# A mixture-of-experts kernel: routing sums and tables in another order, the scatters in another order, fewer table steps, longer warm-up

## What is computed

```python
x = x + xattn(_layernorm(x), ctx, ctx, lens, ...)
xf = _layernorm(x)                                   # 2048 tokens, 256 wide
probs = softmax(einsum('td,ed->te', xf, gate_w))     # 8 experts
weights, idx = top_k(probs, 2)
weights = weights / sum(weights)
x1 = silu(einsum('td,efd->tef', xf, w1))             # 512 wide
x3 = einsum('td,efd->tef', xf, w3)
out_all = einsum('tef,edf->ted', x1 * x3, w2)
x = x + einsum('tkd,tk->td', take(out_all, idx), weights)
```

## Time and profile before

| | us |
|---|---|
| median of 3 runs | 1250.87 (1248.97 to 1251.0) |
| profiled execution | 1252.28 |
| its span in the profile | 1250.5 |
| TensorE busy | 1092.7 (87%) |
| VectorE busy | 978.4 (78%) |
| ScalarE busy | 729.5 (58%) |
| GpSimd busy | 654.2 (52%) |

### The profile page before, as it was taken

One profiled execution on the slowest core, in us unless ns is written; L12 is line 12 of the kernel. 1 busy time (PEld: TensorE's weight loads), 2 busy tenths in 40 slices (PEclk: granted clock), 3 DMA queues, 4 the chain that ended last, 5 costly groups with the idle time before them and its releaser, 6 DMA issues. The chain is left out here.

```text
span 1250.5 us, 33103 instructions
## 1 busy us (share of the span) xinstructions
PE 1092.7 (87%) x13015; PEld 711.6 (57%) x13015; DVE 978.4 (78%) x1781; ACT 729.5 (58%) x1297; POOL 654.2 (52%) x466
## 2 busy tenths in 40 slices
PE   1455999999999999999999999999978945999996
PEld 0322556656656656655665665666647942666663
DVE  5835899899999989989999999989944763555553
ACT  2522666666666666666666666666644642555553
POOL 1043684486477367448647746844349544333332
PEclk9656999999999999999999999999998976999999
DMA  8024232423333253242333324316636522333330
GB/s 271 1 54 104 77 85 57 123 71 96 87 89 82 62 130 84 62 109 75 91 94 89 86 70 114 86 41 182 206 113 236 169 86 76 56 50 55 52 59 11
DMA packets 103968, 117.03 MB, mean 94 GB/s; under 512 B 47293, under 2 KB 86014, under 8 KB 102526
## 3 DMA queue, kind: packets, MB, share of 16 engines
q1 hardware_dynamic: 91406, 100.46, 28.9%
q0 software_dynamic: 7152, 8.43, 4.0%
q10 hardware_dynamic: 5248, 5.92, 1.6%
HBM read 39.46 MB, written 36.87 MB: 61 GB/s over the span
## 5 line engine op out<-in xcount | busy, mean ns | idle before, releaser
L771 ACT ACTIVATE prob<-sc,key_bias 128x512 f32<-128x512 f32 x640 | 404.8, 684 | 149.4 <-PE sc L634 145.6
L852 DVE TENSOR_REDUCE part_max<-mx 128x1 f32<-128x427 f32 x768 | 418.4, 592 | 49.8 <-PE mx L646 49.8
L949 POOL TENSOR_TENSOR prob_lo<-prob 128x1024 bf16<-128x1024 f32 x128 | 242.2, 1893 | 240.3 <-ACT prob L771 240.3
L864 DVE TENSOR_TENSOR prob_lo<-prob 128x1024 bf16<-128x1024 f32 x192 | 274.7, 1431 | 10.8 <-ACT prob L771 7.2
L673 PE MATMUL pv<-VV,prob 128*128 128x65 bf16 x2560 | 268.0, 193 | 3.7 <-POOL prob_lo L949 3.5
L675 PE MATMUL pv<-VV,prob_lo 128*128 128x65 bf16 x2560 | 269.3, 195 | 0.0
L674 PE MATMUL pv<-VV,prob 128*128 128x64 bf16 x2560 | 268.0, 193 | 0.0
L673 PEld LDWEIGHTS pv<-VV,prob 128*128 128x128 bf16 x2560 | 239.8, 99 | 38.8 <-POOL prob_lo L949 7.3
L674 PEld LDWEIGHTS pv<-VV,prob 128*128 128x128 bf16 x2560 | 237.2, 97 | 26.5
L646 PE MATMUL mx<-K,Q 128*128 128x427 bf16 x768 | 237.2, 350 | 11.4 <-DMA K<-we 6.1
L633 PE MATMUL sc<-Q,K 128*128 128x512 bf16 x640 | 243.6, 381 | 1.3 <-ACT prob L771 1.3
(11 more groups left out here) (182 smaller groups left out, 1453.8 us busy)
## 6 DMA issues: line engine op xcount, KB each, us to landing
expert_inputs<-zeros SPq DMA_DIRECT2D x129, 129.0 KB, 2.8
Q<-we SPq DMA_DIRECT2D x48, 256.0 KB, 4.0
we<-in_w_exp SPq DMA_DIRECT2D x8, 1536.0 KB, 8.3
q32s<-q SPq DMA_DIRECT2D x128, 64.0 KB, 2.0
attention_out<-o_out SPq DMA_DIRECT2D x64, 128.0 KB, 1.9
o_in<-attention_out SPq DMA_DIRECT2D x16, 512.0 KB, 3.8
K<-we SPq DMA_DIRECT2D x48, 160.0 KB, 3.8
VV<-next_v SPq DMA_DIRECT2D x16, 322.5 KB, 4.1
```

Source lines behind the costliest of these rows:

```text
L771: act.activation(prob[:, s % PRING, j, :], sc[n % 2][:], ACT.Exp, bias=key_bias[:, t:t + 1], scale=HD ** -0.5).then_inc(exp_done, 1)
L852: dve.tensor_reduce(part_max[:, b_ % 2, qt, h:h + 1], mx[:, pl.part_banks(qt, h)[0]:pl.part_banks(qt, h)[-1] + 1, 0:pl.width], mybir.AxisL ...
L864: dve.tensor_tensor(prob_lo[:, s % PRING, 0:g, :], prob[:, s % PRING, 0:g, :], hi_half(prob[:, s % PRING, 0:g, :])[:, :, 1::2], ALU.subtra ...
L949: pool.tensor_tensor(prob_lo[:, s % PRING, 0:g, :], prob[:, s % PRING, 0:g, :], hi_half(prob[:, s % PRING, 0:g, :])[:, :, 1::2], ALU.subtr ...
```

## The change

The change touches four engines.

- *TensorE.* `places` is split into `places_from` (earlier tiles) and `places_within` (the batch's own), `counts` into tiles 0 to 11 and 12 to 15. Of batch 3 only the own part and the last four counts wait for its choice. `warm_up` has 17 products instead of 9 and doesn't wait for the low scatters.
- *VectorE.* Both choices lie in one tile `picks`, so that `place` has one product and one reduce for both; the minimum and maximum are written as whole numbers at once. `weights` is split into `shares`, `weigh_low` and `weigh_high`. `shares(3)` and `weigh_high(2)` move between `choose(3)` and `place(3)`, `weigh_high(3)` behind the tables. The tables (`tables`, before `owners`) have 14 steps instead of 19, and where two steps don't depend on each other the first is not waited for (`note`).
- *GpSimd.* Batch 1's high scatters move behind batch 3's low ones. The last twelve high scatters go in bursts of four, each waiting for the ones before.
- *SyncE* waits for `tables_made`, reads the entries of two tiles, loads these, and then reads and loads tile by tile.

```diff
@@ SyncE
-                sp.wait_ge(owner_made, 1)
+                sp.wait_ge(tables_made, 2)
                 sp.sem_inc(load_turn, 1)
-                first = [place_of(i) for i in range(TURN)]
+                first = [place_of(i) for i in range(2)]
                 for c in range(CH):
                     sp.wait_ge(scattered_low[c], 16 * QT)
-                for i in range(TURN):
+                for i in range(2):
                     fetch(i, *first[i])
+                for i in range(2, TURN):
+                    fetch(i, *place_of(i))
...
@@ GpSimd
-                def scatter_high(c, paced=False):
+                def set_high(c):
                     pool.wait_ge(scattered_low[c], 16 * QT)
                     pool.wait_ge(high_weighted, c + 1)
                     pool.tensor_copy(row_weights[:, batch(c)], high_weight[:, batch(c)]).then_inc(high_weights_set, 1)
                     pool.wait_ge(high_weights_set, c + 1)
-                    for t in range(c * QT, (c + 1) * QT):
-                        if paced and t % 2 == 0:
+
+                def scatter_high(tiles_, paced=False):
+                    for t in tiles_:
+                        if paced and t % QT == 0:
                             pool.wait_ge(scattered_high, 16 * t)
...
+                EARLY = QT
                 for c in range(CH - 2):
                     scatter_low(c)
-                    scatter_high(c)
+                    set_high(c)
+                    scatter_high(range(c * QT, min((c + 1) * QT, EARLY)))
                 for c in range(CH - 2, CH):
                     scatter_low(c)
...
+                scatter_high(range(EARLY, 2 * QT), True)
                 for c in range(CH - 2, CH):
-                    scatter_high(c, True)
+                    set_high(c)
+                    scatter_high(range(c * QT, (c + 1) * QT), True)
...
@@ VectorE
-                    for k in range(2):
-                        then(dve.tensor_tensor(g8[k][:], slot_of[:], pick[k][:], ALU.mult))
-                        then(dve.tensor_reduce(slot_f[:, k, :], g8[k][:], AX_X, ALU.add))
-
-                    then(dve.tensor_tensor(slot_f[:, 2, :], slot_f[:, 0, :], slot_f[:, 1, :], ALU.min))
-                    then(dve.tensor_tensor(slot_f[:, 3, :], slot_f[:, 0, :], slot_f[:, 1, :], ALU.max))
-                    dve.tensor_copy(slot[:, :, batch(c)], slot_f[:, 2:4, :]).then_inc(slots_made, 1)
...
+                    then(dve.tensor_reduce(slot_f[:].rearrange("p k t -> p (k t)"),
+                                           picked_slots[:].rearrange("p k t e -> p (k t) e"), AX_X, ALU.add))
+
+                    dve.tensor_tensor(slot[:, 0, batch(c)], slot_f[:, 0, :], slot_f[:, 1, :], ALU.min).then_inc(slots_made, 1)
+                    dve.tensor_tensor(slot[:, 1, batch(c)], slot_f[:, 0, :], slot_f[:, 1, :], ALU.max).then_inc(slots_made, 1)
+                    note(dve.tensor_tensor(first_low[:, c % 2, 0, :], slot_f[:, 0, :], slot_f[:, 1, :], ALU.is_lt))
+                    then(dve.tensor_tensor(first_low[:, c % 2, 1, :], slot_f[:, 0, :], slot_f[:, 1, :], ALU.is_gt))
...
                 place(2)
-                weights(2)
+                shares(2)
+                weigh_low(2)
                 keep_logits(3)
                 choose(3)
+                shares(3)
+                weigh_high(2)
                 place(3)
-                weights(3)
-                owners()
+                weigh_low(3)
+                tables()
+                weigh_high(3)
...
@@ TensorE
-                places(3)
                 pe.wait_ge(x1_made, ST)
-                for t in range(ST):
-                    ins = pe.matmul(counts, ones_b[:], chosen[:, t, :], start=t == 0, stop=t == ST - 1)
-                ins.then_inc(counted, 1)
+                count_tiles(range(0, 3 * QT))
+                pe.wait_ge(pc_read, 3)
+                places_from(3, range(3 * QT), True)
+                pe.wait_ge(chosen_made, 4)
+                places_within(3, False)
+                count_tiles(range(3 * QT, ST)).then_inc(counted, 1)
...
                 pe.wait_ge(owner_made, 1)
-                pe.wait_ge(scattered_low[CH - 1], 16 * QT)
-                warm_up(9)
+                warm_up(17)
```

More of the change, by code:

```diff
@@ L1498, in owners, with weigh_high, tables @@
+                def weigh_high(c):
+                    note(dve.tensor_tensor(ew_part[:, 2, :], ew[:, c % 2, 2, :], first_low[:, c % 2, 1, :], ALU.mult))
+                    then(dve.tensor_tensor(ew_part[:, 3, :], ew[:, c % 2, 3, :], first_low[:, c % 2, 0, :], ALU.mult))
+                    dve.tensor_tensor(high_weight[:, batch(c)], ew_part[:, 2, :], ew_part[:, 3, :], ALU.add).then_inc(high_weighted, 1)
+                def tables():
                     dve.wait_ge(counted, 1)
-                    then(dve.tensor_copy(count[:], counts))
@@ L1512, in owners @@
-                    then(dve.tensor_copy(owner[:], owner_f[:, 1, :]))
+                    dve.tensor_scalar(scatters[:], tile_numbers[0:1, :], tiles[0:1, 2, 0:1], 1.0, ALU.is_ge, ALU.add).then_inc(tables_made, 1)
+                    dve.wait_ge(picked, chain[0])
                     then(dve.tensor_tensor(skipped[:], ended[:, :, 0:E - 1],
                                            tiles[0:1, 3, 0:E - 1].unsqueeze(1).to_broadcast([1, MT, E - 1]), ALU.mult))
-                    then(dve.tensor_reduce(row_f[:, 0, :], skipped[:], AX_X, ALU.add))
@@ L1517, in owners @@
-                    then(dve.scalar_tensor_tensor(out=row_f[:, 1, :], in0=tile_numbers[0:1, :], scalar=float(P), in1=row_f[:, 0, :],
+                    note(dve.tensor_reduce(row_f[:, 0, :], skipped[:], AX_X, ALU.add))
+                    then(dve.tensor_reduce(owner_f[:], ended[:], AX_X, ALU.add))
+                    note(dve.scalar_tensor_tensor(out=row_f[:, 1, :], in0=tile_numbers[0:1, :], scalar=float(P), in1=row_f[:, 0, :],
                                                   op0=ALU.mult, op1=ALU.add))
-                    then(dve.tensor_scalar(row_f[:, 2, :], row_f[:, 1, :], float(E * S), None, ALU.min))
@@ L1520, in owners @@
-                    then(dve.tensor_copy(tile_row[:], row_f[:, 2, :]))
-                    then(dve.tensor_scalar(scatter_f[:, 0, :], tile_numbers[0:1, :], tiles[0:1, 2, 0:1], None, ALU.is_ge))
-                    then(dve.tensor_scalar(scatter_f[:, 1, :], scatter_f[:, 0, :], 1.0, None, ALU.add))
-                    dve.tensor_copy(scatters[:], scatter_f[:, 1, :]).then_inc(owner_made, 1)
+                    dve.tensor_scalar(owner[:], owner_f[:], float(E - 1), None, ALU.min).then_inc(owner_made, 1)
@@ L1526, in _ @@
+                    dve.wait_ge(picked, chain[0])
+                    dve.tensor_scalar(tile_row[:], row_f[:, 1, :], float(E * S), None, ALU.min).then_inc(tables_made, 1)
                 for step in range(STEPS):
@@ L1552, in _ @@
                     if step in (2 * QT + 3, 3 * QT + 3):
-                        weights((step - 3) // QT - 2)
+                        shares((step - 3) // QT - 2)
+                        weigh_low((step - 3) // QT - 2)
+                        weigh_high((step - 3) // QT - 2)
                     if step == ST + 1:
@@ L1611, in _, with mine, places_from, places_within @@
             def _(pe):
+                def mine(c):
+                    return pc[:, c * QT * E:(c + 1) * QT * E]
+                def places_from(c, tiles_, start):
+                    for t in tiles_:
+                        pe.matmul(mine(c), ones_b[:], chosen[:, t:t + 1, :].to_broadcast([P, QT, E]),
+                                  start=start and t == tiles_.start, stop=False)
+                def places_within(c, start):
+                    pe.matmul(mine(c), before_b[:], chosen[:, batch(c), :].rearrange("p t e -> p (t e)"), start=start, stop=False)
+                    for t in range(c * QT, (c + 1) * QT - 1):
+                        ins = pe.matmul(mine(c)[:, (t + 1 - c * QT) * E:QT * E], ones_b[:],
+                                        chosen[:, t:t + 1, :].to_broadcast([P, (c + 1) * QT - 1 - t, E]),
+                                        start=False, stop=t == (c + 1) * QT - 2)
+                    ins.then_inc(pc_ready, 1)
                 def places(c):
```

88 lines of the change are left out of this document (42 added, 46 removed).

## The result

| | before | changed |
|---|---|---|
| median (us) | 1250.76 (1248.97 to 1251.0) | 1242.18 (1241.82 to 1243.91, 4 runs) |
| ratio | 1 | 0.9944 [0.9929, 0.9960] |
| span of the profiled execution | 1250.5 | 1242.1 |

Faster by 8.6 us by the medians and by 7.0 by the ratio. The prediction was 1239.4 with a range of 1235.5 to 1243: right in direction and in what sets the end, 2.8 us too fast by the median and 4.5 by the ratio (0.9944 x 1250.87 = 1243.9, just outside the range). One term of its sum was too small, the waits between bursts of scatters.

The account below looks back on a forecast made before the run. Everything between the last routing batch and TensorE's first real tile was taken as exposed. Afterwards the stores set the end: first store -9.8, chain -1.7, so 1250.87 - 11.5 = 1239.4 us, range 1235.5 to 1243.

Parts of the forecast that it names:

- Earlier batches, -0.5: VectorE's batch 1 weights ahead of the residual add lose three chained steps: 0.5 us saved, ends 0 and -0.7.
- VectorE's steps (-1.5, -2.6, -1.5): Savings in us: batch 2 from place to next logits; batch 3's wait between choice and place; batch 3 from place to low weights.
- tables (6.0 to 4.0): VectorE's stretch from batch 3's low weights to finished tables shrinks from 6.0 to 4.0 us.
- The stall, taken as 0: Part of VectorE's 3.83 us wait for batch 3's sums might travel to the remaining matmuls: bounds 0 and +2.4 us.
- First load -12.9: SyncE's first tile load, released by batch 3's low scatters, comes at 1032.4 instead of 1045.35 us.
- Warm-up -2.2: Seventeen throwaway products raise TensorE's clock, so the first tile's 12 matmuls take 2.7 us instead of 4.89.
- The store chain sets the end: Stores end 11.5 us earlier, less than TensorE's 15.1, so GpSimd's scatters and stores decide the end.
- with 2.06 to 2.62 of waiting between bursts (2.3 taken, twice): GpSimd's waits between the bursts of four late high scatters, ahead of the first store: 2.3 us each.
- The chain itself, -1.7: From first to last store: 1.7 us less, the middle between -2.8 and -0.6.
- Shared interfaces, 0.1 a scatter: VectorE and GpSimd contending for SBUF might make each scatter 0.1 us longer, 1.6 over sixteen.
- Rival 1: Stores keep up and TensorE sets the end: -15.1 us, 1235.8; chance 0.15.
- Rival 2: The stall travels: batch 3's place waits 2.4 us longer, scatters and first store follow, 1241.8; chance 0.18.

Follow-up runs that it names:

- after_again: The changed kernel run again with no edit, for a second trace; its end came 228.9 us after batch 2's logits.
- sums_late: Changed kernel with all of batch 3's sums on TensorE behind its choice again; the end came 2.3 to 3.5 us later.
- sync_undone: Changed kernel with SyncE reading all twelve table entries ahead of the first load again; ratio 0.9955, end 5.5 to 6.7 us later by trace.
- sync_only: Kernel before with only SyncE's change: entries of two tiles read and loaded first, the others one by one; ratio 0.9963 [0.9947, 0.9979].
- before_again: The kernel before run again with no edit, for a second trace; it repeated within 0.5 us from batch 2's logits on.
- store_late: Changed kernel with four chained clears on GpSimd between the last scatter's landing and the first store; ratio 0.9945, end 3.3 to 4.5 us later.
- pairs: Changed kernel with the twelve late high scatters in bursts of two instead of four; ratio 0.9996 [0.9981, 1.0011], end 237.1 us after batch 2's logits.
- loads_held: Changed kernel with SyncE holding the loads of tiles 2 to 5 until all scatters have landed; ratio 1.0030 [1.0016, 1.0043].
- warm25: Changed kernel with 25 throwaway products instead of 17; its end came 228.2 us after batch 2's logits.
- early8: Changed kernel with batch 1's high scatters back ahead of batch 2's low ones; ratio 0.9928, end 226.0 us after batch 2's logits.
- early8_held: Changed kernel with batch 1's high scatters early again and loads of tiles 2 to 5 held until all scatters landed; end 231.5 us after batch 2's logits.

## Why the prediction was right or wrong

The sum, by its own terms, from the logits of batch 2 (forecast 1012.5):

```
                                forecast   changed   after_again
logits(2), absolute              1012.5    1014.4    1012.7
low weights of batch 3             12.4      12.6      12.4
first load                         19.9      20.7      19.9
last high scatter ends             37.2      39.3      38.6
first store                        39.8      42.0      41.2
first to last store               177.6     176.7     178.7
end                               226.5     227.7     228.9
```

- **Earlier batches, -0.5: not tested.** In the profiled execution the logits came 1.45 later, not 0.5 earlier, but the kernel before's own two traces differ by 2.9 at this place (1012.95 and 1015.89). In 1009.50 to 1012.90 the clock was at 0.50 and the last projection took 3.40 us and more at it. The dip is in three traces (changed, sums_late, sync_undone) of the kernels with the new routing and in none of the others, before among them. Whether the change makes it likelier is open: 3 of 11 such traces against 0 of 3.
- **VectorE's steps (-1.5, -2.6, -1.5) and tables (6.0 to 4.0): right** within 0.3 us each.
- **The stall, taken as 0: right for this kernel** (the wait is gone in all ten traces with the sums made early), but my reading of its cost was incomplete. It isn't a fixed price: with the sums behind the choice, choice to place took 4.1, 3.6 and 4.0 us in three traces, and 0.9 in sync_only. So "-2.6" is what the change is worth on the executions that have the stall. The cause that I suspected was an incoming block of instructions (`q8 instruction: 1, 0.02`), which in before moved at 1025.0, in the middle of the wait. In sync_only it moved at 1021.3, 0.9 us after the short wait was over, so that trace can't test it. before_again speaks against it: it waited 3.32 us, and its trace records no such block from 1015 to 1040. Nor are TensorE's products late: by their rows, whose ends are modelled, the sums ended at 1024.59 in before, 3.2 us ahead of VectorE's next step, and the releaser named is `remote`, not TensorE. The cause stays open.
- **First load -12.9: right** (from the logits -12.4 forecast, -11.7 and -12.5 measured). The last step to it, landing and issue of the load, took 1.9 in the forecast and 2.4 in the first trace, where the low scatters ended at 1032.67 (0.31 ahead of the first high one).
- **Warm-up -2.2: right in one trace, not in the other.** The clock rose as forecast. I had not asked what happens between the last throwaway product and the first tile: 2.94 us idle, then the dip. Tile 0's result came 11.8 earlier and 14.5 earlier in the two traces; forecast 14.6 from the logits. The 2.7 us between them did not reach the end.
- **The store chain sets the end: right**, shown by store_late and pairs. **Its head was mis-sized:** the step that failed is "with 2.06 to 2.62 of waiting between bursts (2.3 taken, twice)". From the end of one burst to the start of the next it took 2.99 and 3.48 (6.5 in all), and 5.8 in the second trace, against 4.6: +1.2 to +1.9 on the first store. In the four other traces with this order of scatters it took 4.9 to 6.4. Of that 0.4 are two copies of the high weights, which I had left out. The rest, 0.8 to 1.5 in the changed kernel's traces, are longer landings, and why they are longer is open: the loads are not shown to do it (loads_held), nor is the size of the bursts, for bursts of two waited 1.92 to 3.88 in pairs. The bounds were too narrow even by the trace that they came from, which has a third wait between bursts that I didn't use:

```profile
1051.48 0.96 POOL L1397 DMA_INDIRECT expert_inputs<-yrows,slot  x1 [2.77 <-DMA expert_inputs<-yrows,slot]
```

- **The chain itself, -1.7: right as a middle.** -2.6 and -0.6: the two ends that I had worked out both occurred. At the very end gaps were 3.6, shorter than the 4.2 taken.
- **The sign "nearly all stores released by the store before": met**, though the view gives only 28 of 39 in the first trace (see the result).
- **Shared interfaces, 0.1 a scatter: not seen.** Beside VectorE's choice, slots and tables the eight low scatters of the first trace took 0.96 to 0.98, one of them 1.12.
- **A slip of the text:** it is batch 1's high scatters that no longer stand ahead of batch 3's low ones, not batch 2's. The moments worked out don't change.
- **Rival 1 (TensorE sets the end): refuted** for the changed kernel by pairs, by warm25 and by after_again. In the first trace it came within 1.5 us of being true, and in the kernels with early scatters it is true. **Rival 2** gave almost the measured time (1241.8) for a cause that did not occur.

So of the 3.1 us between forecast and measured span (1239.0, 1242.1), 1.9 stand ahead of the routing and 1.2 behind it: 2.2 lost in the waits and landings up to the first store, 0.9 won back in the store chain, 0.1 rounding. That is one execution, the slowest of the four. In the second trace it is 2.4 behind the logits, 1.4 of them up to the first store. And part of the miss is spread: the same kernel on another chip had a ratio of 0.9922, which would be 1241.1, inside the range and still 1.7 above the forecast.

What each part is worth is known only roughly. By the traces the whole is 8.1 to 9.8; undoing SyncE's reads cost 5.5 to 6.7, of which some is the slow reads of that one execution (by the ratios 1.4 to 4.1); putting the sums late cost 2.3 to 3.5 (by the ratios 1.0 to 3.8). The reads act through the result of tile 0, the sums through the scatters. The reordering of the scatters costs the store chain, and the bursts of four repay it.

## What to carry to other kernels

When an exposed stretch of 13 us is cut, write down the second chain's head row by row as carefully as the first's, its small copies included, and take the bounds of a wait from every row that has one: here it kept back 5 to 7 us of what TensorE had won (result 11.8 and 14.5 earlier, first store 7.2 and 8.0). Test an order of DMAs against both chains: putting scatters behind others gave one engine 1 us and took 6 from the other. And compare traces from an event just ahead of the edit when executions spread over more than the effect.

## What the runs showed of the hardware

- The wait for a burst of four scatters to land spread from 2.2 to 3.6 us over executions of nearly the same program: 2.79 and 3.28 (changed), 3.11 and 2.32 (after_again), 2.49 and 3.55 (sync_undone), 2.23 and 2.30 (sums_late), 2.21 and 2.36 with no loads beside them (loads_held).
- Twelve reads of table entries by SyncE took 8.3 us in two executions and 11.7 in a third.
- The idle gap between the last throwaway product and the first real one varied between executions. Where its row says 1.68, 1.76, 2.20, 2.25 or 2.50 us (after_again, sums_late, pairs, loads_held, store_late), the first tile's 12 matmuls took 2.87, all at 1.00. Where it says 2.94 or 3.32 (changed, early8) they took 4.48, with the granted clock falling to 0.50 in the tile, and where it says 4.71 or 9.08 (early8_held, sync_undone) 5.30, with the clock down before it. All of these had 17 products ahead. In sync_only, with nine products and the clock at 1.00 only at their end, a gap of 1.77 was followed by 4.47 us and a clock of 0.50.
- VectorE's wait behind the same 32 small matmuls was 0.61 us in one execution and 3.83 in another, with no edit near them. A single trace's stall may be no property of the code.
- The Trainium skill, "Runtime: NRT & Kernel Launch", "Instruction fetch mechanics", says that crossing an instruction block is mostly hidden. No run here shows it either way: in before a block moved during the wait of 3.83 us, in before_again none was recorded during that of 3.32, and in sync_only it moved after the wait of 0.61 was over.
